# A quarter of the last batch's fp8 rounding, from VectorE to GpSimd

## The reference, cut to what matters

```
def _div_clamp_fp8(x, scale):
    y = jnp.clip(x.astype(jnp.float32) / scale, -FP8_MAX, FP8_MAX)
    y = y.astype(jnp.bfloat16).astype(jnp.float32)
    return _fp8_roundtrip(y)
```

## Time and profile before

| | us |
|---|---|
| median of 3 runs | 1785.48 (1784.53 to 1785.58) |
| profiled execution | 1783.69, span 1781.8 |
| PE busy | 1737.0 (97%) |
| DVE busy | 1405.0 (79%), 4581 instructions |
| ACT busy | 1105.4 (62%) |
| POOL busy | 273.5 (15%), 428 instructions |

### The profile page before, as it was taken

How to read it: one execution, slowest core, us unless ns; L and a number is a source line. 1 busy time by engine, 2 the same in 40 slices (tenths; PEclk the granted TensorE clock), 3 DMA queues, 4 the chain that set the end, 5 groups by cost and what they waited for, 6 DMA issues and landing times.

```text
span 1781.8 us, 31332 instructions
## 1 busy us (share of the span) xinstructions
PE 1737.0 (97%) x10664; PEld 1183.0 (66%) x10664; DVE 1405.0 (79%) x4581; ACT 1105.4 (62%) x2378; POOL 273.5 (15%) x428
## 2 busy tenths in 40 slices
PE   9999999988999999999999999999999999989998
PEld 4454444666777777777777777777777777744554
DVE  1243526589889998898899899899889988879996
ACT  1252515376577667667666667767667665657776
POOL 0000000211111111112121111111111112101111
PEclk9999999999999999999999999999999999999999
DMA  8212200101101120120121012111101012000000
GB/s 284 83 59 83 71 24 26 37 1 49 50 19 32 49 68 19 44 68 26 37 66 38 19 44 68 37 44 54 32 19 44 32 48 97 1 1 19 25 25 30
DMA packets 45596, 83.30 MB, mean 47 GB/s; under 512 B 3584, under 2 KB 22528, under 8 KB 45056
## 3 DMA queue, kind: packets, MB, share of 16 engines
q1 hardware_dynamic: 45440, 81.31, 14.1%
HBM read 69.77 MB, written 10.49 MB: 45 GB/s over the span
## 4 chain that ended last, share of the span: by engine, by line
PE 64%; DVE 20%; issue 9%; ACT 3%; POOL 3%; DMA 1%; POOLq 0%; ACTq 0%; DVEq 0%
PE bank L533 14%; PE bank L596 9%; PE bank L642 8%; PE bank L691 5%; PE bank L620 4%; PE bank L727 3%; PE bank L455 3%; PE bank L493 3%; PE bank L575 2%; PE bank L407 2%; DVE nq L1239 2%; PE bank L434 2%; DVE nmx L1389 2%; DVE bnB L1215 2%; PE bank L569 2%
## 5 line engine op out<-in xcount | busy, mean ns | idle before, releaser
L533 PE MATMUL bank<-wqs,XQ 128*128 128x256 f16 x2048 | 245.6, 273 | 5.5 <-DVE x L1270 5.5
L596 PE MATMUL bank<-prT,KV 128*128 128x256 f32 x1024 | 247.5, 385 | 0.0
L642 PE MATMUL bank<-kT,qT 128*128 128x512 f32 x512 | 240.9, 593 | 0.9 <-issue 0.9
L596 PEld LDWEIGHTS bank<-prT,KV 128*128 128x128 f32 x1024 | 190.9, 192 | 73.2 <-issue 52.1
L533 PEld LDWEIGHTS bank<-wqs,XQ 128*128 128x128 bf16 x2048 | 197.6, 98 | 47.3 <-DVE x L1270 21.0
L1009 ACT ACTIVATE pr<-bank,nmx 128x512 f32<-128x512 f32 x256 | 174.4, 688 | 57.2 <-DVE nmx L1389 55.7
L1558 POOL TENSOR_TENSOR rdev<-gvar,cst 128x7 f32<-128x7 f32 x128 | 192.6, 1505 | 10.0
L1556 POOL TENSOR_TENSOR gvar<-mvB,geps 128x7 f32<-128x7 f32 x128 | 30.7, 240 | 1044.8 <-DVE mvB L1229 1044.8
L1389 DVE TENSOR_REDUCE nmx<-bank 128x1 f32<-128x512 f32 x256 | 167.6, 681 | 9.5 <-PE bank L642 7.1
L691 PE MATMUL bank<-identf,pr 128*128 128x128 f32 x1024 | 151.9, 276 | 18.4 <-DVE pr L1249 14.5
L810 ACT ACTIVATE prT<-bank 128x512 f32<-128x512 f32 x256 | 153.1, 614 | 25.7 <-PE bank L691 25.5
(11 more groups left out here) (179 smaller groups left out, 3097.8 us busy)
## 6 DMA issues: line engine op xcount, KB each, us to landing
wst<-in_wcat SPq DMA_DIRECT2D x21, 512.0 KB, 4.0
nq<-in_wgu SPq DMA_DIRECT2D x16, 512.0 KB, 3.5
wpst<-in_wproj SPq DMA_DIRECT2D x8, 1024.0 KB, 6.4
wa<-in_wgu SPq DMA_DIRECT2D x16, 512.0 KB, 3.7
xT<-in_xT SPq DMA_DIRECT2D x4, 1024.0 KB, 7.7
nq<-in_wdn SPq DMA_DIRECT2D x8, 512.0 KB, 3.5
wkx<-in_wkvx SPq DMA_DIRECT2D x8, 512.0 KB, 4.8
tern_gu<-wa SPq DMA_DIRECT2D x16, 256.0 KB, 2.0
```

The lines of the kernel that those rows point to most:

```text
L533: ins = mm(dst, XQ[:, b, c, k, j * P:(j + 1) * P], w, start=(k == 0 and m == 0), stop=(k == KT - 1 and m == 1))
L596: ins = mm(OB[:, 0:2 * P], KV[:, n % 2, t, P:2 * P], prT[:, st % 2, t, :, :].rearrange("p h s -> p (h s)"), start=(t == 0), stop=(t == ST ...
L642: mm(SB_[h][:], qT[:, h, st * P:(st + 1) * P], kT[:, :], start=True, stop=True).then_inc(s["scores_made"], 1)
```

## The change

The fourth quarter (k = 3) of the last batch's rows is clamped, scaled, added to and subtracted from on POOL. Only the mask stays on DVE, in one piece in step 6. POOL clamps in step 5 after its `deviations`; in step 6 after its `deviations` it does max and multiply and the add; in step 7 after its `deviations` the subtract. The helper tile is now `pt`, the second half of `wpst`. PE and SP wait for `xp_ready` in place of the last count of `xq_ready`.

```
-ROUND = {(i // 4, i % 4): ((i - 11) // 5, (i - 11) % 5) for i in range(11, 31)}
+ROUND = {(i // 4, i % 4): ((i - 11) // 5, (i - 11) % 5) for i in range(11, 26)}
+PROUND = {5: (0,), 6: (2, 3), 7: (4,)}
...
+        pt = wpst[:, 2:4, :].rearrange("p k n -> p (k n)").bitcast(BF16).rearrange("p (c s) -> p c s", c=4)
...
                 if g == 1:
-                    sp.wait_ge(s["xq_ready"], KT * NB)
+                    sp.wait_ge(s["xq_ready"], KT * NB - 1)
+                    sp.wait_ge(s["xp_ready"], 1)
...
-                        pe.wait_ge(s["xq_ready"], KT * (n + 1))
+                        pe.wait_ge(s["xq_ready"], KT * (n + 1) - (1 if n == NB - 1 else 0))
+                    if n == NB - 1:
+                        pe.wait_ge(s["xp_ready"], 1)
...
+            def mask_last():
+                dve.wait_ge(s["wp_ready"], 1)
+                dve.wait_ge(s["xp_clamped"], 1)
+                v.tensor_scalar(pt.bitcast(U16), XQ[:, NB - 1, :, KT - 1, :].bitcast(U16), 0x7F80, None, ALU.bitwise_and).then_inc(s["xp_masked"], 1)
...
                     if T:
                         round_terms(T - 1)
+                    if T == 6:
+                        mask_last()
...
+            def quant_pool(i):
+                rows = XQ[:, NB - 1, :, KT - 1, :]
+                if i == 0:
+                    pool.wait_ge(s["xA_out"], 4 * KT * NB)
+                    g.tensor_scalar(rows, rows, FP8_MAX, -FP8_MAX, ALU.min, ALU.max).then_inc(s["xp_clamped"], 1)
+                elif i == 2:
+                    pool.wait_ge(s["xp_masked"], 1)
+                    own.do(g.tensor_scalar(pt, pt, FP8_TINY, FP8_ROUND, ALU.max, ALU.mult))
+                elif i == 3:
+                    own.sync()
+                    own.do(g.tensor_tensor(rows, rows, pt, ALU.add))
+                else:
+                    own.sync()
+                    g.tensor_tensor(rows, rows, pt, ALU.subtract).then_inc(s["xp_ready"], 1)
...
                     if nxt:
                         deviations(4 * n + 4 + st)
+                    if T in PROUND:
+                        for i in PROUND[T]:
+                            quant_pool(i)
```

More of the change, by code:

```diff
@@ L217, in build @@
             gA_out tA_out pA_exp vA_out mA_out xA_out
-            maxA_ready pA_scaled yA_added varA_ready rstdA_ready nbA_ready xl_done xn_ready xq_ready
+            maxA_ready pA_scaled yA_added varA_ready rstdA_ready nbA_ready xl_done xn_ready xq_ready xp_clamped xp_masked xp_ready
             scores_made proj_q_made proj_kv_made kvx_made av_made pt_made qt_made kt_made kxt_made
```

## The result

The changed kernel takes 1795.36 us (median of 4 runs, 1794.62 to 1797.04) against 1785.01 (4 runs, 1784.3 to 1785.58): a ratio of 1.0057, 95% interval 1.0045 to 1.0069, so 10 us slower. The profiled execution took 1797.04 us, its span is 1795.1: 13.3 us over the span of before, more than the 10 of the medians, since it was the longest of its four executions and the one of before, with 1783.69, shorter than all four there.

A forecast was written before the change was run, and what follows sets the result against it. DVE was taken to bound the path before 427.09 us, then mostly PE, 97% busy overall. Blocking by POOL gave 5.8 + 1.0 = +6.8 us on 1785.5, so 1792.3; own range 1789 to 1797, 8 in 10 1784.4 to 1799.

The forecast's parts named there:

- The mechanism: POOL's 2048-column instructions block DVE's double-speed SBUF and two-SBUF-input instructions for their whole length; +3.6 to +11 us, chance 0.50.
- Step 5: POOL's clamp delays DVE's mask of quarter 2 by 2.3 us, less 0.6 saved; PE resumes 1.7 us later.
- Step 7: Max and multiply and the add delay DVE by 7.8 us; less 2.0 slack, PE's transposes come 5.8 us late.
- the bound of 4.2: Upper estimate in us for a one-input POOL instruction on 2048 columns, used for clamp and max and multiply; 2.2 was assumed.
- Step 8: POOL's subtract makes `nq` wait 2 us, half covered by ACT: +1.0 us; PE's wait for `xp_ready` is hidden.
- What the change saves: DVE sheds 3.50 us, but only the clamp's 0.6 lies on the path; up to 1 more by the clock, not counted.
- No blocking: Rival: POOL and DVE do not block each other at this size, only the clamp's -0.6 us remains; 1784.9 us, chance 0.25.
- DVE keeping the port: Rival: POOL gets in only at DVE's PSUM or statistics instructions; +2 to +5 us, 1789, chance 0.14.
- its queue effect: In the rival where DVE keeps the port, the add pushes `deviations` for step 8 behind it; +2 to +5 us in all.
- POOL slow: Rival: POOL's instructions are near their upper bounds; +12 to +18 us, about 1799, chance 0.09.

The follow-up runs named there:

- the shortened instruction: Changed kernel with POOL's max and multiply replaced by min and max, factor left out, so rounding terms are wrong: 1791.76 us for 1784.71, ratio 1.0036.
- the shifted clamp: Kernel before with only quarter 3's clamp on POOL, delayed to run beside DVE's PSUM reads in step 5: 1786.61 us for 1785.46, ratio 1.0002.
- The run with the clamp alone: Kernel before with only quarter 3's clamp on POOL, right behind `deviations` in step 5: 1786.79 us for 1784.77, ratio 1.0009.
- POOL idle: Changed kernel with POOL's clamp, max and multiply, add and subtract of quarter 3 left out: 1782.88 us for 1784.77, ratio 0.9987.
- the pieces: Changed kernel with POOL's max and multiply, add and subtract each split into four instructions of 512 columns, clamp whole: ratio 1.0048.
- the run with POOL alone: Kernel before plus unused POOL instructions of several forms from 20 us on, while DVE is nearly idle: 1795.18 us in one run.
- the run beside DVE: Kernel before plus unused POOL instructions of several sizes at its start, beside rounds of small DVE instructions: 1785.29 us in one run.

## Why the prediction was right

- **The mechanism.** It was right: POOL's instructions of 2048 columns hold DVE's two-port and two-input instructions up. Shown in the profile after (2.13 beside 1.89, 7.25 beside 7.12), by the shortened instruction (2.02 beside 1.89) and by the shifted clamp, which in the rows undoes the stretch without doing less work. One exception: a two-input add beside max and multiply ended 4.75 us into its 7.20. Before, only the opposite direction could be seen.
- **Step 5.** Predicted +2.3 for the clamp with 2.2 us of POOL, less 0.6; it took 1.89 and put DVE back 1.7, by stretching the `round_terms` row that had been counted as done before the clamp. The run with the clamp alone gave +1.2.
- **Step 7.** Here the forecast of 5.8 us late for PE fell short: its first `pr` transposes came 11.94 later than in the earlier trace rows, 9.7 without the 2.3 from before. The mis-sized term is max and multiply: 2.2 assumed, 7.12 measured. I had counted it as a one-input instruction like the clamp, and took the bound of 4.2 as its end; it lies beyond. The two-input ones were right: 4.04 and 4.07 for 4.2. With 7.1 in its place the sum is 6.8 + 4.9 = 11.7, near the local +11.1. A smaller slip stands beside it: I counted PE's slack to the first `pr`, 2.0 us, but PE takes `kn` first and waits for the last `nq`, which had 2.7 us (430.22 to 432.96).
- **Step 8.** +1.0 for the subtract was not there: `nq` grew by 0.9 us (2.03), but DVE then waited 0.97 for ACT as before. In its place PE was 1.4 us slower from 445.34 to 455.18 (9.84 us for 8.45), after its long wait, with a granted clock of 0.71 from 432 to 446 us and 0.89 from 446 to 456. These 1.4 and the 9.7 of step 7 are the local 11.1. The wait for `xp_ready` was hidden as forecast: the subtract ended at 452.62, PE came to it at 456.54.
- **What the change saves.** I said 0.6 us, perhaps up to 1 more by the clock, and counted none of the latter. With POOL idle it is 1.9, 0.5 of it from DVE and the rest from the clock. In the changed kernel the same matmuls are as fast, but PE then stands 9.60 us, so that nothing of it is left.
- **The rivals.** No blocking: fallen. DVE keeping the port: fallen, since POOL's clamp ran from 415.54 inside an unbroken run of DVE and put DVE back, and the add ran ahead of three `nq`. But its queue effect is real once DVE isn't blocked, as the pieces showed. POOL slow: half true, for one of four instructions.

The whole time, 1795.36, is 3.1 us over the 1792.3 predicted. That it lies inside the forecast's own 1789 to 1797 is in part luck: one term was short by 4.9 us, and about 1 us in step 7 and the 1.0 of step 8 that was not there made up for some of it, while the clock in step 8 added 1.4.

## What to carry over

Before work goes from DVE to POOL, write down which DVE instructions will stand beside it and what they read: beside DVE's PSUM instructions and reductions it was free; a two-port instruction beside a POOL instruction of 2048 columns lasted to POOL's end, and so did a two-input one, but for the add beside max and multiply. Price each POOL operation by its own row, since forms that look alike differ by almost four times, and look where small stages behind it in its queue are due. A DVE row in such a profile that grows to the length of the POOL row beside it is a wait, though the page books it as busy.

## What the runs showed of the hardware

- POOL on 128x2048 bf16: min and max together 1.88 us, max alone 5.37, multiply alone 5.38, max with multiply or with add 7.12 to 7.20, two-input 4.04 to 4.07 with two tiles and 3.60 to 3.66 with one tile as both inputs, memset 1.80 to 1.87. The Trainium skill, GPSIMD Engine Reference, section Engine selection, calls one-input operations roughly line-rate, without a word on which. The trace has 0.9 ns a column for the clamp and 3.5 ns for max and multiply, so that cannot hold for both.
- The port is not always held for the whole instruction. The Trainium skill, SBUF — State Buffer, section Who interferes with whom, says that the shared pair is held for the whole instruction. The trace agrees for two-port instructions of DVE beside 2048 columns (held until 0.08 us after POOL's end); for max and multiply it does not at 1024 (0.8 of 3.64 us), at 512 (0.1 of 2.07 alone, up to 0.4 in the kernel) and at 256 (0.2 of 1.06), and at 2048 a two-input add ended 4.75 us into its 7.20. Two-input pieces of 512 did hold each `nq` up, 1.1 us each. Why the one-input form frees the port earlier was not tried.
- POOL's memset of 2048 columns left a two-input add its 0.28 us and held a two-port multiply to its own end (1.27 us for 0.23). One place of one run shows this.
- In the run with POOL alone, the first instruction but a memset after the partition reduction at 20.24 us began 8.01 us late, at 30.39, with nothing that it waited for. Ahead of the reduction, in the run beside DVE, such instructions started without it.
- The length of a wait of PE does not by itself tell what the clock does behind it: after about 1.99 us the next sixteen matmuls took 1.92 us in four of these kernels, and 3.54 and 3.58 in the clamp-only and short-max runs. What decides was not tried.
